# Banded attention: two masks of eight on GpSimd, value products in pairs, three of four projections inside the loop

## The reference, cut to what matters

```python
def sdpa(q, k, v, mask):
    scores = jnp.einsum('bhqd,bhkd->bhqk', q, k) / np.sqrt(HD).astype(np.float32)
    scores = jnp.where(mask, scores, jnp.float32(-1e+30))
    probs = jax.nn.softmax(scores, axis=-1)
    return jnp.einsum('bhqk,bhkd->bhqd', probs, v)

def local_gqa_attn(x, wq, wk, wv, wo):
    ...                                   # project, rope, normalise q and k, repeat k and v
    i = jnp.arange(x.shape[1])
    diff = i[:, None] - i[None, :]
    mask = (diff >= 0) & (diff < WIN)     # WIN = 32
    return merge_heads(sdpa(q, k, v, mask)) @ wo

x = hidden
x = x + global_latent_attn(rmsnorm(x, norm1_w), g_wq, g_kv_down, g_k_up, g_v_up, g_wo)
x = x + local_gqa_attn(rmsnorm(x, norm2_w), l_wq, l_wk, l_wv, l_wo)
```

## Time and profile before

| | |
|---|---|
| median of three runs | 1798.23 us (1796.87 to 1801.2) |
| the profiled execution: span from first to last instruction | 1795.2 us (the page gives no other time for it) |
| busy over the span: PE, DVE, ACT, POOL | 91%, 55%, 46%, 20% |
| mean granted TensorE clock over the span | 0.951 of full |
| the stage, first scores to last addition | 1506.6 to 1584.5 us of the span |

### The profile page before, as it was taken

The page is one execution under the profiler, slowest core; times in us unless marked ns, Lnnn a source line. Parts: engine busy times, 40 slices in busy tenths (PEclk is TensorE's granted clock), DMA queues, the critical chain, the costliest instruction groups (busy, mean ns, idle before and its releaser), DMA issues. The chain is left out here.

```text
span 1795.2 us, 25021 instructions
## 1 busy us (share of the span) xinstructions
PE 1626.7 (91%) x8797; PEld 881.4 (49%) x8849; DVE 983.2 (55%) x2214; ACT 818.3 (46%) x1338; POOL 354.4 (20%) x492
## 2 busy tenths in 40 slices
PE   7889977999997997999699989998799987979998
PEld 2436653344433664446444555666333344545665
DVE  7663447887772334535553353446633447963444
ACT  5643333566665332433143333222688856743221
POOL 1314232222222523201330032001300100032000
PEclk9989987999998998999899989998899988989999
DMA  4642025010103201000000016553211024105544
GB/s 111 233 131 90 25 74 152 28 55 28 55 2 129 105 30 40 1 1 1 1 0 1 0 32 132 122 124 86 81 48 34 17 52 124 55 31 125 119 112 94
DMA packets 56221, 120.22 MB, mean 67 GB/s; under 512 B 8439, under 2 KB 35095, under 8 KB 51299
## 3 DMA queue, kind: packets, MB, share of 16 engines
q1 hardware_dynamic: 53628, 113.55, 23.3%
q0 software_dynamic: 2432, 5.00, 0.8%
q10 hardware_dynamic: 39, 0.07, 0.0%
HBM read 85.38 MB, written 19.96 MB: 59 GB/s over the span
## 5 line engine op out<-in xcount | busy, mean ns | idle before, releaser
L2471 DVE TENSOR_REDUCE a_most<-psum 128x1 f32<-128x512 f32 (+3 forms) x304 | 181.7, 655 | 31.0 <-PE psum L2317 20.3
L2429 ACT ACTIVATE a_probs<-psum 128x512 f32<-128x512 f32 (+1 forms) x304 | 155.4, 578 | 94.8 <-PE psum L2347 62.6
L3302 ACT ACTIVATE t_silu<-psum 128x512 f32<-128x512 f32 x136 | 81.2, 597 | 240.6 <-PE psum L3360 239.5
L3377 PEld LDWEIGHTS psum<-t_slot,t_hid 128*128 128x128 f32 x1024 | 132.1, 192 | 55.9 <-issue 49.7
L2730 ACT ACTIVATE ga_probs<-psum 128x1024 f32<-128x1024 f32 (+2 forms) x160 | 138.5, 951 | 24.3 <-PE psum L2644 24.2
L3473 DVE TENSOR_TENSOR t_prod<-t_silu,psum 128x512 f32<-128x512 f32 x104 | 71.5, 688 | 137.4 <-ACT t_silu L3302 137.4
L3377 PE MATMUL psum<-t_slot,t_hid 128*128 128x128 f32 x1024 | 134.4, 277 | 3.0 <-DVE t_hid L3464 3.0
L3360 PE MATMUL psum<-xnT,t_slot 128*128 128x512 f32 x256 | 131.2, 594 | 3.1 <-ACT t_silu L3302 3.1
L3365 PE MATMUL psum<-xnT,t_slot 128*128 128x512 f32 x256 | 130.7, 592 | 0.0
L2314 PE MATMUL psum<-a_ks,a_qs 96*128 96x512 bf16 (+3 forms) x384 | 119.7, 342 | 10.5 <-DMA a_qs<-a_most_parts 3.8
L3464 DVE TENSOR_TENSOR t_hid<-t_prod,t_spread 128x512 f32<-128x512 f32 x128 | 89.9, 705 | 37.5 <-DMA t_spread<-factors 31.0
(11 more groups left out here) (453 smaller groups left out, 3007.9 us busy)
## 6 DMA issues: line engine op xcount, KB each, us to landing
t_spread<-factors SPq DMA_DIRECT2D x64, 512.0 KB, 6.4
m_experts<-experts_dram SPq DMA_DIRECT2D x14, 768.0 KB, 9.1
c_halves<-xnT SPq DMA_DIRECT2D x48, 128.0 KB, 2.3
t_slot<-experts_dram SPq DMA_DIRECT2D x32, 192.0 KB, 5.2
a_qs<-scratch_q SPq DMA_DIRECT2D x16, 288.0 KB
a_ks<-scratch_k SPq DMA_DIRECT2D x24, 192.0 KB
ga_qs<-scratch_q SPq DMA_DIRECT2D x16, 288.0 KB
la_qs<-scratch_q SPq DMA_DIRECT2D x16, 288.0 KB
```

What stands on the lines that cost most here:

```text
L2429: act.activation(probs[:, (n * BLOCKS + b) % PROBS, h0:h0 + heads, 0:wide], src, ACT.Exp, scale=SCALE).then_inc(probs_ready, 1)
L2471: v.tensor_reduce(most[:, row, h0:h0 + heads, qt % KPH], src, AX.X, ALU.max).then_inc(max_read, 1)
L3377: ins = pe.matmul(core.psum[:, c, t * P:(t + 1) * P], left[:, t * P:(t + 1) * P], weights, start=pair < 0 and t == 0, stop=False, skip_gro ...
```

## The change

Five edits in `attend_band_stage`:

1. The masks of key blocks 0 and 4 of each group (`kt % SHARE == 0`, `SHARE` = 4) are done by GpSimd, the other six by VectorE. They have a semaphore of their own, `masked_pool`.
2. The four additions of the second branch go from VectorE to GpSimd, after its mask of block 4 in groups 1 to 4.
3. TensorE issues the value products in pairs: scores 0, scores 1, the last two value products of the group before, scores 2, scores 3, value products 0 and 1, and so on. The turns stay after scores 7 and 3, but stand ahead of the pair.
4. Chunks 0 and 1 are transposed, copied and projected at the start of groups 4 and 5 (`PROJECT`), in bank 6, chunk 2 ahead of and behind the last two value products, chunk 3 at the end.
5. VectorE adds a projected chunk after mask 1 of those groups; the first value product of the group waits for it.

```diff
@@ GpSimd, VectorE: a shared helper
+        def mask_probs(engine, n, kt):
+            wide = width(kt)
+            engine.wait_ge(probs_ready, n * KT + kt + 1)
+            part = probs[:, (n * KT + kt) % PROBS, :, 0:wide]
+            return engine.tensor_tensor(part, part, keep[:, 0:wide].unsqueeze(1).broadcast_to([P, G, wide]), ALU.mult)
@@ GpSimd, per group
                 g.tensor_copy(vslot[...], v_all[...]).then_inc(vslot_ready, 1)
+                if n == 0:
+                    g.wait_ge(keep_ready, 1)
+                for kt in range(0, KT, SHARE):
+                    mask_probs(g, n, kt).then_inc(masked_pool, 1)
+                    if n in range(1, NC + 1) and kt == SHARE:
+                        tiles = slice(TPC * (n - 1), TPC * n)
+                        g.tensor_tensor(out[:, tiles, :], out[:, tiles, :], also[:, tiles, :], ALU.add).then_inc(also_added, 1)
@@ TensorE, values
-                pe.wait_ge(masked, n * KT + kt + 1)
+                count = n * KT + kt
+                if kt % SHARE == 0:
+                    pe.wait_ge(masked_pool, count // SHARE + 1)
+                else:
+                    pe.wait_ge(masked, count - count // SHARE)
                 if kt == 0:
                     pe.wait_ge(vslot_ready, n + 1)
+                    if n in (GPB, GPB + 1):
+                        pe.wait_ge(y_added, n - GPB + 1)
@@ TensorE, the loop   (PROJECT = {(GPB, 0): 0, (GPB + 1, 0): 1})
+            def project_turn(c, bank):
+                for t in range(TPC):
+                    ins = pe.transpose(core.psum[:, bank, t * P:(t + 1) * P], otok[:, TPC * c + t, :], core.c("ident"))
+                ins.then_inc(oT_pe, 1)
+            def project(c, bank):
+                pe.wait_ge(oT_ready, c + 1)
+                for t in range(TPC):
+                    ins = pe.matmul(core.psum[:, bank, t * P:(t + 1) * P], core.xnT[:, c * CH + t * P:c * CH + (t + 1) * P], w_out, start=True, stop=True)
+                ins.then_inc(y_pe, 1)
             for n in range(GROUPS):
                 for kt in range(KT):
                     scores(n, kt)
-                    if kt >= LAG:
-                        values(n, kt - LAG)
-                    elif n:
-                        values(n - 1, KT - LAG + kt)
+                    if (n, kt) in PROJECT:
+                        if n == GPB:
+                            pe.wait_ge(w_out_in, 16)
+                        pe.wait_ge(o_ready, 2 * n - 1)
+                        project_turn(PROJECT[n, kt], O_BANK)
+                    if (n, kt - 1) in PROJECT:
+                        project(PROJECT[n, kt - 1], O_BANK)
                     if kt == TURN_A:
                         turn(n, 0)
                     if kt == TURN_B and n:
                         turn(n - 1, 1)
+                    if kt % LAG == LAG - 1:
+                        for k in range(kt - LAG - 1, kt - 1):
+                            if k >= 0:
+                                values(n, k)
+                            elif n:
+                                values(n - 1, KT + k)
+            pe.wait_ge(o_ready, 2 * GROUPS - 1)
+            project_turn(NC - 2, O_BANK)
             for kt in range(KT - LAG, KT):
                 values(GROUPS - 1, kt)
+            project(NC - 2, O_BANK)
             turn(GROUPS - 1, 1)
...
             pe.wait_ge(o_ready, 2 * GROUPS)
-            ...                                  # the four chunks' transposes, then their projections
+            project_turn(NC - 1, O_BANK + 1)
+            project(NC - 1, O_BANK + 1)
@@ ScalarE, after the exponential of (n, kt)
+                    if (n, kt) in PROJECT:
+                        copy_turned(PROJECT[n, kt], O_BANK)
...
+            copy_turned(NC - 2, O_BANK)
             copy_o(GROUPS - 1, 1)
+            copy_turned(NC - 1, O_BANK + 1)
@@ VectorE
+            def add(c, bank):
+                v.wait_ge(y_pe, c + 1)
+                v.wait_ge(also_added, c + 1)
+                ...                              # out += projected chunk c
             for n in range(GROUPS):
                 for kt in range(KT):
-                    ...                          # mask of every block; in groups 1 to 4 out += also
+                    if kt % SHARE:
+                        mask_probs(v, n, kt).then_inc(masked, 1)
+                    if (n, kt - 1) in PROJECT:
+                        add(PROJECT[n, kt - 1], O_BANK)
...
+            add(NC - 2, O_BANK)
             normalise(GROUPS - 1, 1)
+            add(NC - 1, O_BANK + 1)
```

More of the change, by code:

```diff
@@ L2824, in attend_band_stage @@
     WIDE = P + window
+    SHARE = 4
+    PROJECT = {(GPB, 0): 0, (GPB + 1, 0): 1}
     COPY_A, TURN_A, NORM_A = KPH + 1, KT - 1, KT - 1
@@ L2841, in attend_band_stage @@
         masked = core.sem(ctx, tag + "masked")
+        masked_pool = core.sem(ctx, tag + "masked_pool")
         pv_pe = core.sem(ctx, tag + "pv_pe")
@@ L2981, in _ @@
                         copy_o(n - 1, 1)
+            copy_turned(NC - 2, O_BANK)
             copy_o(GROUPS - 1, 1)
-            for c in range(NC):
-                act.wait_ge(oT_pe, c + 1)
-                act.activation(core.xnT[:, c * CH:(c + 1) * CH], core.psum[:, c % 2, :], ACT.Copy).then_inc(oT_ready, 1)
+            copy_turned(NC - 1, O_BANK + 1)
         @block.vector
@@ L2998, in normalise @@
                 v.tensor_tensor(dst, turned[:, :, :, 0:HD], sums[:, :, :].unsqueeze(3).broadcast_to([P, KPH, G, HD]), ALU.mult).then_inc(o_ready, 1)
+            def add(c, bank):
+                v.wait_ge(y_pe, c + 1)
+                v.wait_ge(also_added, c + 1)
+                tiles = slice(TPC * c, TPC * (c + 1))
+                y = core.psum[:, bank, :].rearrange("p (t d) -> p t d", d=D)
+                v.tensor_tensor(out[:, tiles, :], out[:, tiles, :], y, ALU.add).then_inc(y_added, 1)
             v.wait_ge(masks_in, 16)
@@ L3007, in _ @@
                 for kt in range(KT):
-                    wide = width(kt)
-                    v.wait_ge(probs_ready, n * KT + kt + 1)
-                    part = probs[:, (n * KT + kt) % PROBS, :, 0:wide]
-                    v.tensor_tensor(part, part, keep[:, 0:wide].unsqueeze(1).broadcast_to([P, G, wide]), ALU.mult).then_inc(masked, 1)
-                    if n in range(1, NC + 1) and kt == KPH:
-                        tiles = slice(TPC * (n - 1), TPC * n)
-                        v.tensor_tensor(out[:, tiles, :], out[:, tiles, :], also[:, tiles, :], ALU.add).then_inc(also_added, 1)
+                    if kt % SHARE:
+                        mask_probs(v, n, kt).then_inc(masked, 1)
+                    if (n, kt - 1) in PROJECT:
+                        add(PROJECT[n, kt - 1], O_BANK)
                     if kt == NORM_A:
@@ L3018, in _ @@
                         normalise(n - 1, 1)
+            add(NC - 2, O_BANK)
             normalise(GROUPS - 1, 1)
-            v.wait_ge(also_added, NC)
-            for c in range(NC):
-                v.wait_ge(y_pe, c + 1)
-                tiles = slice(TPC * c, TPC * (c + 1))
-                y = core.psum[:, 2 + c % 2, :].rearrange("p (t d) -> p t d", d=D)
-                v.tensor_tensor(out[:, tiles, :], out[:, tiles, :], y, ALU.add).then_inc(y_added, 1)
+            add(NC - 1, O_BANK + 1)
 def channels_stage(core, w4, w4_in, xr, tag, norms):
```

17 lines of the change are left out of this document (3 added, 14 removed).

## The result

The changed kernel takes 1805.89 us (median of 9 runs, 1803.96 to 1817.04), the kernel before 1799.03 beside it on the same chip (9 runs, 1794.51 to 1803.62). The ratio is 1.0043, 95% interval 1.0027 to 1.0060: 5 to 11 us slower, clear of no change, though the interval's lower end (0.27%) lies inside the 0.3% that the prediction took as no change. 1806.8 was forecast.

The account below looks back on a forecast made before the run. The prediction took TensorE to set the pace, VectorE just behind. Its terms, +2.9 + 1.8 + 6.0 - 2.1 = +8.6 us on the profiled span of 1795.2, gave span 1803.8 and time 1806.8, range 1790 to 1815.

Parts of the forecast that it names:

- first group: First group: VectorE's splitting of the last projection meets GpSimd's mask 0; taken as 0 (+-0.5) us.
- Part 1: Paired value products: eight of sixteen changes leave TensorE, 0.72 us a group, a gain only while TensorE sets the pace.
- Part 2: Masks 0 and 4 on GpSimd: 1.54 us each, blocking VectorE's next mask; a group takes 8.15 us, +2.9 in all.
- Part 3: Second branch's four additions on GpSimd: VectorE's masks 6 and 7 wait, 0.95 us a group; net +1.8.
- Part 4: Projections 0 and 1 in groups 4 and 5: TensorE waits for the normalised half; +3.0 us each, +6.0.
- Part 5: End of the stage: 7.6 us behind the last mask instead of 9.7, -2.1.
- the port is free: Rival on the masks: GpSimd and VectorE don't hold each other up; -6.4 us, 1791.8; chance 0.17.
- the walk: Step-by-step timing of one head group from the end of exponential 0; 8.15 us from exponential 0 to exponential 0.
- the third rival: TensorE's granted clock falls after new waits of 1 to 3 us; four to six spells, +6, 1813; chance 0.13.
- The projections are cheap: Rival on the loop's two projections: 1.45 us each, or hidden; +5.5 to +2.6 in all, about 1802; chance 0.17.

Follow-up runs that it names:

- e5: The changed kernel with GpSimd's masks replaced by zero fills of its own array, blocks 0 and 4 left unmasked: 1799.41 us, ratio 1.0002.
- e8: The kernel before with one edit, the value products in pairs: 1794.35 us, ratio 0.9988.
- e11: As e10, with value products four to five blocks behind the scores, six probability buffers, and copies, turns and normalised halves moved along: 1790.35 us, ratio 0.9958.
- e4: The kernel before with one edit, the masks of blocks 0 and 4 on GpSimd: 1807.23 us, ratio 1.0048.
- e6: The changed kernel with chunks 0 and 1 transposed and projected behind the loop, in banks the scores have left: 1798.72 us, ratio 1.0004.
- e3: The changed kernel with the transposes and projections of chunks 0 and 1 behind scores 2 of groups 4 and 5: 1803.71 us, ratio 1.0027.
- e9: The changed kernel with the four additions back on VectorE, in front of its mask 5: 1804.01 us, ratio 1.0034.
- e10: The changed kernel with all masks and additions on VectorE and chunks 0 and 1 projected behind the loop: 1791.81 us, ratio 0.9971.
- e1: The changed kernel with all masks on VectorE, GpSimd keeping only the additions: 1799.35 us, ratio 1.0003.

## Why the prediction was right, step by step

The time was right to 0.9 us, and part of that is luck. The difference between the kernels was forecast at 8.6 us and measured at 6.9; the base of the forecast, 1798.2, lay 0.8 below the median that the kernel before had beside the changed one, and two terms of the sum were off in opposite directions. From the table, forecast against measured: first group 0 and -0.5; parts 1 and 2 +2.9 and 7 x (8.14 - 7.79) = +2.5; part 3 +1.8 and -0.6; part 4 +6.0 and +7.5; part 5 -2.1 and 7.55 - 9.68 = -2.1. The sums are +8.6 and +6.8; the stages differ by 6.7.

**Part 2, masks on GpSimd: right, mechanism and size.** GpSimd's mask takes 1.54 us where nothing delays it, the forecast to the hundredth, and the blocked one ends 0.68 us behind it (0.69). The halves between GpSimd's masks are 4.11 and 4.02 us long, a plain group 8.14 (8.15). The rival "the port is free" asked for VectorE masks all near 0.82 and groups of 7.3: out. e5 is the direct evidence: the same length of GpSimd work without the reads leaves VectorE's masks at 0.83. The rule that the prediction took from the Trainium skill, "SBUF — State Buffer", section "SBUF: two separate sides", agrees; it limits the case of two SBUF inputs to a GpSimd operation that reads SBUF, and e5's 0.83 agrees with that too. The slot copy, which the walk let move masks 6 and 7 by up to 0.5 us, costs the mask behind it 0.04 (0.85 us against 0.81).

**Part 1, pairs: used up, as said, but not worth 0.72.** Eight changes did leave TensorE (0.55 us of busy time in e8), but without GpSimd's masks a plain group gains 0.15, because another floor sits just below, by the waits and e11 the chain copy, turn, normalise, value product 3. The prediction named TensorE as what sets the pace of the kernel before, with "VectorE just behind"; the next limit was neither engine's work but, as far as the runs show, this chain. The sum did not need it, since GpSimd's masks set a higher floor (8.15). Against that, e4 shows that without the pairs part 2 would have cost 1.06 us more a group.

**Part 3, additions on GpSimd: over-sized.** Groups with one were to be 0.95 us over a plain one, net +0.46 each; they are 0.33 over it (8.47), net -0.16, so +1.8 should have been about -0.6, the other sign. The step that failed is the start of the walk to it, "mask 7 moves from 8.25 to 9.30". In the trace masks 5 to 7 take 3.05 us and end at 1577.12, 0.5 ahead of GpSimd's next start at 1577.63: the walk had both at 8.25. With an addition they take 4.04:

```profile
1541.45 4.04 DVE L2865 TENSOR_TENSOR la_probs<-la_probs,la_keep 128x640 f32<-128x640 f32 x3 [0.39 <-ACT la_probs L3011]
1542.40 1.77 POOL L2894 TENSOR_TENSOR x<-x,xn_row 128x512 f32<-128x512 f32 x1
...
1544.12 0.83 POOL L2887 COPY la_vslot<-l_v_all 128x64 f32<-128x64 f32 x1
1545.01 1.88 POOL L2865 TENSOR_TENSOR la_probs<-la_probs,la_keep 128x640 f32<-128x640 f32 x1
...
1546.13 0.63 PE L2950 MATMUL psum<-const,la_otok 128*128 128x128 f32 x4 [2.00 <-DVE la_otok L3035]
1546.80 0.60 ACT L2999 ACTIVATE xnT<-psum 128x512 f32<-128x512 f32 x1 [1.86 <-PE psum L2950]
1547.45 1.84 PE L2956 MATMUL psum<-w,xnT 128*128 128x128 f32 x8 [0.41 <-ACT xnT L2999]
1549.22 1.19 PE L2937 MATMUL psum<-la_probs,la_vslot 128*32 128x160 f32 x16
```

Half of the added microsecond falls into that gap. GpSimd's next mask still starts on time behind the copy (1545.01, 4.11 behind the one before, as in the plain group) and only lasts 1.88 us instead of 1.54, as VectorE's mask 7 runs until 1545.49: the 0.34 by which the group is longer. "Mask 7 moves" was right, "the next mask 0 and 1 with it" was not.

**Part 4, projections in the loop: right in kind, under-sized.** +6.0 was forecast, 3.0 each; against e6 the two cost 3.11 in group 5 and 4.42 in group 4. The rows above show the chain that the prediction wrote down: TensorE idle 2.00 us for the normalised half, ScalarE's copy 0.67 behind the transposes, 0.41 more for that copy, and the two value products behind it all. Group 5 is that, to 0.1 us. What group 4 has over it is the granted clock, 0.87 in its window, and in a narrower one of the kernel after 0.67, part of it at 1.2 GHz:

```profile
1546.10:1551.20 5.10, 4.66 (x41) 3.73 (x42) 1.51 (x2) 1.84 (x4) 0.79 (x1) 0.67 0.17 45
```

The projection takes 1.84 us there and 1.16 in group 5, the two value products 1.19 and 0.75. This is the third rival, but one spell worth some 1.3 us (4.42 - 3.11) in place of four to six. e5 has it in group 4 too: clock 0.86, and 4.72 us over its groups 2 and 3, against 3.10 in group 5. Group 5 waits as long, at a clock of 1.00:

```profile
1559.02 0.66 PE L2950 MATMUL psum<-const,la_otok 128*128 128x128 f32 x4 [1.99 <-DVE la_otok L3035]
...
1560.37 1.16 PE L2956 MATMUL psum<-w,xnT 128*128 128x128 f32 x8 [0.41 <-ACT xnT L2999]
```

"The projections are cheap" (1.45 each) is out: even without the wait (e3) or with half of it (e9) they cost 2.4 to 2.7, since TensorE's order puts the exponentials' scores behind the chain, as the prediction held against it.

**Part 5, the end: right.** Only chunks 0 and 1 are projected inside the loop; chunk 2's projection stands behind it, around the last two value products, and chunk 3's after that. 7.55 us from the last mask, 7.6 forecast, with the same order: the chunk 2 transposes wait 1.26 us for their half, behind the last projection there is only the last addition.

```profile
1582.20 3.02 DVE L2865 TENSOR_TENSOR la_probs<-la_probs,la_keep 128x640 f32<-128x640 f32 x3 [0.38 <-ACT la_probs L3011]
1585.77 0.66 PE L2950 MATMUL psum<-const,la_otok 128*128 128x128 f32 x4 [1.26 <-DVE la_otok L3035]
...
1590.89 1.16 PE L2956 MATMUL psum<-w,xnT 128*128 128x128 f32 x8 [0.69 <-ACT xnT L2999]
1592.08 0.69 DVE L3042 TENSOR_TENSOR x<-x,psum 128x512 f32<-128x512 f32 x1 [2.59 <-PE psum L2956]
```

Half of this gain doesn't need projections in the loop: with all of them behind it the tail is 17.0 in e10, against 18.6 in e8 with the old end and 15.4 in e1. (The four projections of the kernel before take 7.05 us by the earlier trace rows, 1577.44 to 1584.49, and not 7.2; no term uses it.) The first group, taken at 0 +- 0.5, came out at -0.54, for no reason that a run shows.

## What to carry to other kernels

Moving a two-input product from VectorE to GpSimd freed VectorE of next to nothing here, where VectorE's own work beside it also reads two SBUF tiles (0.82 us taken off, 0.85 added): look in the trace for one place where the two meet, and take the blocked length from there. Work that is put into an in-order stream costs its whole chain of waits and what stands behind it, not its own duration; put it where its input is old, and where the next engine has its work already issued. And an engine that is busy 95% of a group need not be the next floor: here it took longer distances between dependent steps (e11), not less work.

## What the runs showed of the hardware that was not expected

- The hold-up goes the other way too, and the kernel before already had it. GpSimd's one-input copy of 64 columns lasts 0.24 us where no VectorE mask runs. Issued during a mask, it ends 0.10 us behind that mask: after 0.51 us in the kernel before, 0.84 in the kernel after. The rows below are of e5, without a mask, and of the kernel before, where the first mask of the row at 1551.95 ends at 1552.77:

```profile
1566.53 0.23 POOL L2888 COPY la_vslot<-l_v_all 128x64 f32<-128x64 f32 x1
...
1552.36 0.51 POOL L2878 COPY la_vslot<-l_v_all 128x64 f32<-128x64 f32 x1 [7.77 <-PE psum L2915]
```

- TensorE's waits of 2.00 and 0.41 us were followed by a spell with the granted clock at 1.2 GHz in group 4, and waits of 1.99 and 0.41 in group 5, with the same order of work, were not. In e5 waits of 1.45 and 0.41 in group 4 were followed by such a spell; after 1.06 and 0.41 (e9) the clock stayed at 1.00.
- Kernels with the same code up to there had a granted clock of 0.66 (the kernel after, e3, e9) or 0.53 (e6) in the first group, worth 1.0 us (10.02 and 11.05).
